# The last local attention in another order: back products ahead of the counting products, and each chunk's counting, positions and scatters one round later

## What is computed

```python
# step 7, W_a and W_c of L3
score = jnp.einsum('nqh,hk,nlk->nql', decoder_h_t, W_a, encoder_outputs)   # decoder_h_t = layernorm(x)
score = jnp.where(mask[:, None, :], -1000000000.0, score)                  # window around p_t
align = jax.nn.softmax(score, axis=2) * gauss[:, None, :]
context = jnp.einsum('nql,nlh->nqh', align, encoder_outputs)
x = x + jnp.tanh(jnp.concatenate([context, decoder_h_t], axis=2) @ W_c.T)
# step 8
router_probs = jax.nn.softmax(xt @ Wr + br, axis=-1)                       # xt = layernorm(x)
gates, idx = jnp.max(router_probs, axis=-1), jnp.argmax(router_probs, axis=-1)
x = x + gates * (relu(layernorm(xt) @ W1[idx] + b1[idx]) @ W2[idx] + b2[idx])
```

## Time and profile before

| | |
|---|---|
| median of 3 runs | 878.08 us (875.97 to 883.4) |
| profiled execution | 886.11 us, of which the span from the first to the last instruction is 884.3 us |
| PE busy | 701.1 us, 79% of the span |
| DVE busy | 458.7 us, 52% |
| ACT, POOL busy | 249.4 us, 224.5 us |
| mean granted TensorE clock | 0.854 of full speed |

### The profile page before, as it was taken

One profiled execution on the slowest core, in us unless ns is written; L12 is line 12 of the kernel. 1 busy time (PEld: TensorE's weight loads), 2 busy tenths in 40 slices (PEclk: granted clock), 3 DMA queues, 4 the chain that ended last, 5 costly groups with the idle time before them and its releaser, 6 DMA issues.

```text
span 884.3 us, 13677 instructions
## 1 busy us (share of the span) xinstructions
PE 701.1 (79%) x4525; PEld 450.2 (51%) x4525; DVE 458.7 (52%) x1374; ACT 249.4 (28%) x393; POOL 224.5 (25%) x289
## 2 busy tenths in 40 slices
PE   4789999999998997952999457889977867538950
PEld 3664454444444554540999423455433757518950
DVE  6567757575666554456222135264255366654532
ACT  1223232232233331310444202033413722313410
POOL 4710010101142115054000367231210054530024
PEclk9769999999999998775999757699979985559985
DMA  9904221313306000011222110000000050011112
GB/s 359 394 15 160 80 85 51 129 62 98 96 9 278 2 1 24 2 36 51 57 73 61 52 40 21 19 2 1 1 1 1 2 190 1 24 36 58 40 46 83
DMA packets 35781, 60.62 MB, mean 69 GB/s; under 512 B 5377, under 2 KB 21505, under 8 KB 34562
## 3 DMA queue, kind: packets, MB, share of 16 engines
q1 hardware_dynamic: 32642, 53.46, 17.3%
q0 software_dynamic: 3072, 6.30, 2.5%
HBM read 42.83 MB, written 16.91 MB: 68 GB/s over the span
## 4 chain that ended last, share of the span: by engine, by line
PE 61%; DVE 14%; issue 10%; POOL 8%; ACT 3%; DMA 2%; SPq 1%; another core or an unknown queue 1%; DVEq 0%; POOLq 0%; ACTq 0%
PE banks L338 57%; POOL rows_in L2133 3%; POOL SHARE L2115 2%; PE banks L345 2%; POOL XN L2017 1%; DVE stats L993 1%; DVE mx L1405 1%; POOL rstd L2010 1%; PE banks L779 1%; PE banks L906 1%; DMA SHARE<-rows_out,slots 1%; DVE SHARE L1022 1%; DVE mv L998 1%; DVE SHARE L1289 1%
## 5 line engine op out<-in xcount | busy, mean ns | idle before, releaser
L2010 POOL TENSOR_TENSOR rstd<-veps,neghalf 128x4 f32<-128x4 f32 (+1 forms) x32 | 35.7, 1117 | 385.7 <-DVE veps L1004 385.7
L338 PE MATMUL banks<-U 128*128 128x128 f32 (+3 forms) x816 | 124.4, 391 | 1.8 <-ACT U L1882 0.9
L338 PE MATMUL banks<-XNT,SLOT 128*128 128x512 f32 x256 | 122.0, 599 | 0.0
L338 PEld LDWEIGHTS banks<-U 128*128 128x128 f32 (+3 forms) x816 | 82.8, 183 | 11.3 <-issue 10.1
L2115 POOL DMA_INDIRECT SHARE<-rows_out,slots x48 | 45.9, 956 | 167.8 <-DMA rows_out<-SHARE 151.5
L1405 DVE TENSOR_REDUCE mx<-banks 128x8 f32<-128x616 f32 x64 | 51.2, 799 | 68.0 <-PE banks L338 52.0
L1776 ACT ACTIVATE SHARE<-banks,SM 128x512 f32<-128x512 f32 x68 | 46.7, 687 | 136.4 <-PE banks L338 136.4
L338 PEld LDWEIGHTS banks<-XNT,SLOT 128*128 128x128 f32 x256 | 48.7, 192 | 62.4 <-issue 62.2
L1289 DVE SCALAR_TENSOR_TENSOR SHARE<-banks,SM,SHARE 128x512 f32<-128x512 f32 x64 | 48.0, 750 | 51.3 <-PE banks L338 47.2
L338 PE MATMUL banks<-SHARE,SLOT 128*128 128x512 f32 x128 | 67.1, 606 | 3.4 <-DVE SHARE L1293 3.3
L1816 ACT ACTIVATE U<-banks 103x1536 f32<-103x1536 f32 x32 | 46.4, 1450 | 80.3 <-PE banks L338 80.3
(11 more groups left out here) (286 smaller groups left out, 1085.2 us busy)
## 6 DMA issues: line engine op xcount, KB each, us to landing
SLOT<-gates SPq DMA_DIRECT2D x128, 128.0 KB, 2.9
rows_in<-U SPq DMA_DIRECT2D x1, 8192.0 KB, 27.7
SLOT<-l1w SPq DMA_DIRECT2D x2, 2048.0 KB, 13.7
SLOT<-f SPq DMA_DIRECT2D x2, 2048.0 KB, 15.8
U<-rows_in SPq DMA_DIRECT2D x64, 64.0 KB, 1.8
SLOT<-l3w SPq DMA_DIRECT2D x2, 2048.0 KB, 7.7
rows_out<-SHARE SPq DMA_DIRECT2D x14, 256.0 KB, 2.3
SLOT<-w SPq DMA_DIRECT2D x1, 2048.0 KB, 12.8
```

The lines of the kernel that those rows point to most:

```text
L338: return nc.tensor.matmul(out_, lhsT, rhs, start=start, stop=stop, **kw)
L2010: power = g.tensor_tensor(rstd[:, a, 0:w], veps[:, a, 0:w], neghalf[:, 0:w], ALU.pow)
```

## The change

No instruction is added or taken away. Four things move, all under `ahead`, so in the last local attention alone. On PE, `back(i-1)` comes ahead of `prep_xt(28+c)`, and `count` of a chunk leaves the end of its round for the next round, behind `back`. On DVE, `finish` of a chunk leaves the end of its round for the next one, between `prep_ln` and `route`; that of the last chunk stands behind the loop. On ACT, the copy of the transposed rows goes behind the exponential and the tanh. POOL's and SP's lists are as they were.

```diff
@@ PE, window_layer
                     if i - 1 < BATCH:
                         turn_back(i - 1)
+                        back(i - 1)
+                    if ahead and 1 <= c <= BATCH:
+                        count(c - 1)
                     if ahead and 0 <= c < BATCH:
                         prep_xt(4 * (s + 1) + c)
-                    if i - 1 < BATCH:
-                        back(i - 1)
-                    if ahead and 0 <= c < BATCH:
                         logits(c)
                     if i + 1 < BATCH:
                         front(i + 1)
...
-                    if ahead and 0 <= c < BATCH:
-                        count(c)
@@ DVE, window_layer
+                    if ahead and c >= 1:
+                        finish(c - 1)
                     if ahead and c >= 0:
                         route(c)
                         for step in range(4):
...
                     if ahead and c >= 0:
                         choose(c, 4)
-                        finish(c)
...
+                if ahead:
+                    finish(BATCH - 1)
@@ ACT, window_layer
-                    if ahead and 0 <= c < BATCH:
-                        prep_xt(4 * (s + 1) + c)
...
                     if i - 1 < BATCH:
                         back(i - 1)
+                    if ahead and 0 <= c < BATCH:
+                        prep_xt(4 * (s + 1) + c)
```

## The result

The change made the kernel slower by 0.66%: the ratio is 1.0066 (95% interval 1.0039 to 1.0093), some 5.8 us of 878; 20 runs of the changed kernel have the median 886.6 us, 20 of the one before 877.26. The ratio leaves out runs that took over 1.5% more than the fastest of their kernel, 6 of the 20 of the changed kernel, which is why it gives less than the 9.3 us between the medians. The forecast was 883.0 and +4.9 us.

A forecast was written before the change was run, and what follows sets the result against it. It took hand-overs, with no engine full, to bound the stretch from 721.9 to 792.1. Two waits on POOL, the first partly covered, summed to +4.9 us on the 878.08 median: 883.0, range 880.7 to 885.8.

The forecast's parts named there:

- Rival A: On POOL, a scatter does not hold up the next power, so DVE goes on: not slower, 877.0 us; chance 0.10.
- B: On POOL, issues are lengthened by `choose`'s small two-input operations, so waits grow: +7.9 us, 886.0; chance 0.10.
- S: Time of a scatter's four issues on POOL, part of each wait: taken as 4.8 us.
- D: On POOL, `scatter(2)` ends after `slots_in(3)`, a third wait: above +8.8 us, 887 or more; chance 0.03.
- C: PE is granted 2.4 GHz for `back(2)` and the last transposes and router products: +1.5 us, 879.6; chance 0.05.
- Round 2: `choose(0)` starts 0.9 us sooner, limited by ACT's copy of chunk 27's rows; `masked(3)` starts at 750.7.
- Round 3: `add(2)` comes 1.1 us sooner; late `finish(0)` puts `slots_in(0)` at 759.6, behind `veps` of chunk 30.
- my bound of 1.9: If PE were granted 2.4 GHz through `back(2)`, `slots_in(0)` would come 1.9 us sooner.
- The wait: DVE's `scale_ln` waits for POOL's power behind a scatter, twice: 7.7 us from `slots_in` (7.5 to 8.5).
- The gap g: Idle time on POOL between the last issue and the power: 0.3 us, ends 0.1 and 0.65.
- What covers it: Round 4: the late tanh covers part of the first wait; nothing covers the second, `scale_ln(31)` +4.9 us.
- Round 5 and behind: `finish(2)`, 1.29 us, falls into DVE's 2.53 us wait for `logits(3)`, costing nothing; the later chain shifts as a whole.

The follow-up runs named there:

- e2: Changed kernel with only GpSimd's list altered, each scatter a round later behind the next chunk's power; stretch 60.25 us, ratio to before 0.9992.
- e5: Changed kernel with `finish(c-1)` on VectorE moved ahead of `add(i-1)`, GpSimd's list unchanged; stretch 61.38 us, ratio to before 0.9936.
- e6: Changed kernel plus three memsets of an unused tile on GpSimd ahead of the powers of chunks 30 and 31; stretch 69.34 us, ratio to before 1.0021.
- e9: Changed kernel with only the first scatter moved on GpSimd, behind the power of chunk 30; stretch 64.70 us, ratio to before 0.9961.
- e10: Changed kernel with only the second scatter moved on GpSimd, behind the power of chunk 31; stretch 61.93 us, ratio to before 0.9932.
- e7: Kernel before plus three 128x512 memsets on GpSimd ahead of the powers of chunks 30 and 31; stretch 65.01 us, ratio to before 0.9977.
- e11: Kernel before plus 14 single-element memsets on GpSimd ahead of the powers of chunks 30 and 31; stretch 62.28 us, ratio to before 0.9999.

## Why the prediction was right

The sign, the cause and the range were right, and the cause is shown, not argued: without the late scatters on GpSimd the loss turns into a gain (e2), `finish` ahead of `veps` does the same (e5), and a delay on GpSimd is paid twice (e6). Rival A (GpSimd is not held) fell with the profile after, where the power starts behind the fourth issue (769.75); B (longer issues) fell with S = 4.93 and 4.82 us; D (a third wait) did not come: GpSimd was idle for 2.63 us between the third group of issues and the fourth. C, the clock, did not come where C had it: `back(2)` took 3.8 us and the last round's transposes and router products 1.09 and 1.87, all at 1.2 GHz. It came elsewhere, in rounds 2 and 3.

By its steps, against s times of the changed kernel:

- *Round 2.* `choose(0)` was put 0.9 sooner than before, because the copy of chunk 27's rows "cannot move". It did, by 1.7 us (s 23.06, before 24.78): `logits(0)` started 0.5 sooner than before and took 1.06 us at 2.4 GHz, the granted clock of 748 to 753 being 0.84. The first row is of the kernel before, the others are of the changed one:

```profile
743.86 1.85 PE L338 MATMUL banks<-SM,XNT 128*128 128x8 f32 x8
...
749.77 1.06 PE L338 MATMUL banks<-SM,XNT 128*128 128x8 f32 x8 [0.66 <-ACT XNT L1707]
...
748.00:753.00 5.00, 3.56 (x25) 3.06 (x24) 4.15 (x18) 2.35 (x7) 0.94 (x1) 0.84 0.00 0
```

- *Round 3.* The term mis-sized. `slots_in` of chunk 0 was put at s 37.7 and came at 35.69, 2.0 sooner, just past my bound of 1.9. `turn_back(2)` started 2.3 sooner than I had it, since the router's products, chunk 27's transposes and its scores were all drawn forward and partly at the higher clock. `back(2)` itself ran at the lower clock, so the bound of 1.9, which rested on it, was nearly enough by luck.
- *The wait.* 7.7 us from `slots_in` to `scale_ln` were forecast, 7.54 measured in the first round and 7.41 in the second. The gap g is 0.02, not 0.3; S is 4.93 and 4.82, not 4.8.
- *What covers it.* That the first wait would be mostly covered by the late tanh, and the second not, was right: 1.4 and 4.4 us (e9, e10, counted from `slots_in` of chunk 0).
- *Round 5 and behind.* `finish(2)` went into the wait for `logits(3)` (2.52 us), as forecast, and the end followed rigidly.

In sum +4.9 was forecast for the stretch and +2.6 measured there, the lower end of the range: 2.0 of the 2.3 between are the moment of `slots_in` of chunk 0, the rest mostly the shorter waits. The time moved by 5.8 (3.4 to 8.2), which is nearer to the forecast than its working deserves: that is luck. The 3.2 us between are not settled. From the first expert product on the two profiles agree, and ahead of the stretch the program is the same, while the memset of `carry` stood anywhere from 709.0 to 743.4 over all profiled kernels. From the first expert product on it is 92.1 to 92.3 us in nine of the fourteen profiles and 93.5 to 95.0 in the other five, though the program there is the same too. That points to the executions and not to the change, but no run shows it, and whether the stretch without a profile grows by more than 2.6 was not tried.

## What to carry to other kernels

When a step moves by a round, look up every engine that it releases, and ask what stands behind the released instruction in that engine's own list: here an untouched list held a 1.7 us power behind a scatter that was now released too late. A wait's length is not its price; ask what would have been late anyway, and take waits away one at a time to see. Where the whole time scatters by more than the effect, measure the stretch between two rows that the change encloses.

## What the runs showed of the hardware

- GpSimd needs 0.8 us from `slots_in` to its first indirect DMA and 4.8 to 4.9 us for four, but the next instruction on its list starts 0.02 us behind the last issue.
- A memset of 128x512 on GpSimd (0.57 us) held five of six VectorE operations of 128x4 that ran beside it, 0.17 us otherwise, to 0.45 to 0.57; memsets of a single element, 14 in 2.0 us, did not (e7, e11). A filler put in to measure a delay can be a cost of its own.
- The same order of TensorE's work was granted 2.4 GHz in different places in different executions, and the stretch moved by up to 1 us with it: `logits(0)` took 1.85 us in the kernel before and 1.04 in e11, stretch 63.17 and 62.28.
